# A Mamba block and a mixture of experts on one core: orders written out for head and tail, weights loaded at the start, and identity products on TensorE

## The reference

```python
xn = layernorm(x)
u, res = silu((xn @ W_in)[..., :256]), (xn @ W_in)[..., 256:]
delta = softplus(u @ W_delta + b_delta)
Bm, Cm = u @ W_B, u @ W_C                       # 16 states
h[t] = exp(delta[t] * A) * h[t-1] + delta[t] * Bm[t] * u[t]
y[t] = sum over the states of h[t] * Cm[t]
x = x + ((y + u * D) * silu(res)) @ W_out

xn = layernorm(x)
gate = xn @ Wg.T + bias; weights = softmax over the 4 largest of 8
out = swiglu(xn, Ws1, Ws2, Ws3) + sum over e of weights[e] * swiglu(xn, W1[e], W2[e], W3[e])
x = x + out                                     # hidden width 341 per expert
```

## Time and profile before

| what | us |
|---|---|
| median of three runs | 1600.95 (1597.64 to 1606.98) |
| profiled execution | 1600.77 |
| its span | 1598.9 |
| TensorE busy, whole span | 1466.7 (92%) |
| VectorE busy, whole span | 1443.5 (90%) |
| first scan of tile 0 starts | 47.77 |
| first `x1T` (tile 0's expert half begins) | 196.8 |

### The profile page before, as it was taken

How to read it: one execution, slowest core, us unless ns; L and a number is a source line. 1 busy time by engine, 2 the same in 40 slices (tenths; PEclk the granted TensorE clock), 3 DMA queues, 4 the chain that set the end, 5 groups by cost and what they waited for, 6 DMA issues and landing times.

```text
span 1598.9 us, 30425 instructions
## 1 busy us (share of the span) xinstructions
PE 1466.7 (92%) x9216; PEld 1210.6 (76%) x9216; DVE 1443.5 (90%) x2884; ACT 1210.7 (76%) x1789; POOL 848.4 (53%) x509
## 2 busy tenths in 40 slices
PE   3255699999999999999999999999999999999998
PEld 1133378878888887878888887878888798878887
DVE  0789899999999999999999999999999999998443
ACT  3464678888888888888888888978888888884332
POOL 1848474665546374665646385655737484661000
PEclk9567799999999999999999999999999999999999
DMA  4312121201212121201212121111212121100000
GB/s 149 112 41 79 41 80 41 74 14 47 81 41 87 41 87 41 71 16 40 86 41 86 40 83 38 55 38 40 86 41 86 41 79 36 64 23 10 6 7 7
DMA packets 50458, 86.97 MB, mean 54 GB/s; under 512 B 4647, under 2 KB 32804, under 8 KB 50340
## 3 DMA queue, kind: packets, MB, share of 16 engines
q1 hardware_dynamic: 50340, 85.66, 16.2%
HBM read 80.93 MB, written 4.72 MB: 54 GB/s over the span
## 4 chain that ended last, share of the span: by engine, by line
PE 57%; issue 14%; POOL 9%; DVE 8%; ACT 7%; DMA 2%; SPq 1%; DVEq 0%; POOLq 0%; ACTq 0%
PE eo_bank L889 18%; PE turn L836 8%; PE h L873 8%; PE h L875 7%; PE h L874 7%; POOL hb L452 5%; DVE hb L650 4%; PE side L800 3%; ACT L511 2%; PE side L813 2%; PE side L806 2%; DMA bbc<-b_rows 2%; DVE acc L662 2%; POOL soft L445 1%; POOL delta L440 1%
## 5 line engine op out<-in xcount | busy, mean ns | idle before, releaser
L452 POOL TENSOR_TENSOR hb<-soft,bbc 128x1024 f32<-128x1024 f32 x256 | 619.6, 2441 | 250.0 <-PE turn L836 207.5
L889 PEld LDWEIGHTS eo_bank<-w_sb,gated 128*128 128x128 f32 x3840 | 467.5, 192 | 34.8 <-issue 16.0
L889 PE MATMUL eo_bank<-w_sb,gated 128*128 128x128 f32 x3840 | 488.4, 276 | 5.0 <-DVE o L738 3.1
L662 DVE SCALAR_TENSOR_TENSOR acc<-turn,c_sb,acc 128x256 f32<-128x256 f32 x960 | 404.8, 471 | 10.2 <-PE turn L836 8.6
L511 ACT ACT_TABLE_LOAD x297 | 381.1, 1283 | 5.2
L836 PE MATMUL turn<-ident,hb 128*128 128x128 f32 x2048 | 313.6, 282 | 69.5 <-DVE acc L662 37.7
L836 PEld LDWEIGHTS turn<-ident,hb 128*128 128x128 f32 x2048 | 251.4, 145 | 130.8 <-issue 54.7
L594 ACT ACTIVATE s<-h 128x512 f32<-128x512 f32 x384 | 221.7, 596 | 150.9 <-PE h L875 144.0
L650 DVE TENSOR_TENSOR_SCAN hb<-decay,hb 128x512 f32<-128x512 f32 x256 | 330.2, 1317 | 5.0 <-issue 5.0
L650 DVE TENSOR_TENSOR_SCAN hb<-decay_bank,hb 128x512 f32<-128x512 f32 x256 | 310.0, 1211 | 20.5 <-POOL hb L452 13.5
L726 DVE TENSOR_TENSOR gated<-h,s 128x512 f32<-128x512 f32 x384 | 254.8, 676 | 47.3 <-PE h L875 35.1
(11 more groups left out here) (86 smaller groups left out, 1408.4 us busy)
## 6 DMA issues: line engine op xcount, KB each, us to landing
bbc<-b_rows SPq DMA_DIRECT2D x128, 512.0 KB, 5.7
x_in<-x_dram SPq DMA_DIRECT2D x16, 256.0 KB, 3.0
x_cur<-x_dram SPq DMA_DIRECT2D x16, 256.0 KB, 3.3
out_dram<-o SPq DMA_DIRECT2D x16, 256.0 KB, 2.4
gated<-w_all_dram SPq DMA_DIRECT2D x2, 1534.5 KB, 7.3
w_sb<-w_all_dram SPq DMA_DIRECT2D x5, 192.0 KB
b_rows<-cbT SPq DMA_DIRECT2D x16, 32.0 KB, 1.6
w_in_sb<-w_in_dram SPq DMA_DIRECT2D x1, 256.0 KB, 3.2
```

The costliest lines, as they stand in the source:

```text
L452: pool.tensor_tensor(hb[:, arg % HB_RING, :, :], du[:, h, :].unsqueeze(1).broadcast_to((P, GN, TOK)), bbc[:, r, :].rearrange("p (n t) -> p ...
L662: dve.scalar_tensor_tensor(acc[:, blk, :], turn_bank[pair][:, i * DI:(i + 1) * DI], c_sb[:, blk, n:n + 1], acc[:, blk, :], ALU.mult, ALU.add)\
L889: mm = pe.matmul(eo_bank[:, blk * P:(blk + 1) * P], gated[:, k % GATED_RING, blk * P:(blk + 1) * P], w3_sb[:, pair, :], start=(n == 0), st ...
```

## The change

There are five edits.

1. **Orders of their own.** The strings of the loop body stay as they are. Each engine gets two more strings, head and tail, with a tile number at each step, and `bodies` runs head, loop, tail. The loop now runs for j = 6 to 14, nine times in place of eight.
2. **One semaphore per kind of use of `side`,** in place of one for all.
3. **Early loads.** ScalarE issues W1 and W2 at its start, on its own DMA queue, W2 into a second staging buffer, `stage2`, which is the upper half of `hb`. `cut_hi` of W1 now follows `wi.1` of tile 0, `cut_hi` of W2 follows `soft`. VectorE makes both low parts one after the other after `c` of tile 0. GpSimd's `dbu` 4 to 7 of tile 0 wait until both are made. W3 is issued by SP after the last `bbc` of tile 0.
4. **Fewer waits at the start.** GpSimd waits no more for the small loads. VectorE negates A after `ln` of tile 0, not before, and only the first decays wait for it.
5. **Identity products.** TensorE multiplies the identity with itself (128 columns, fp32, into an expert bank that nobody reads yet): 16 times before it waits for the small loads, and then ahead of each step, until the first `h1`: 6 times ahead of `xT` and `dz`, 4 ahead of `bt`, 3 ahead of `wi` and `turn`, 2 ahead of the others.

```diff
+FILLERS = {"xT": 6, "dz": 6, "bt": 4, "wi": 3, "turn": 3}
+SP_HEAD = """
+0:load_x.0 0:b_out.0 0:bbc.0.1.2 0:load_cur.0 1:load_x.0 0:bbc.3 2:load_x.0 0:bbc.4.5.6.7 1:b_out.0
...
+PE_HEAD = """
+0:xT.0 0:wi.0.1 0:bt.0 0:dz.0.1 0:turn.0 0:ct.0 0:turn.1.2 0:wi_res.0.1 0:turn.3.4.5.6 1:xT.0 0:turn.7.8 1:wi.0
+0:turn.9.10.11.12.13 1:wi.1 0:turn.14.15 1:bt.0 0:turn.16 1:dz.0 0:turn.17 1:dz.1
+0:turn.18.19.20.21.22.23.24.25.26.27.28.29.30.31 1:turn.0 0:yT.0.1 1:turn.1 1:ct.0 1:turn.2 0:wo.0 1:turn.3
...
+2:bt.0 2:dz.0 1:turn.20 2:dz.1 1:turn.21.22.23.24 0:x1T.0 1:turn.25.26 0:h1.0.1 1:turn.27 0:h2.0 1:turn.28.29.30
...
+ACT_HEAD = """
+0:xn.0 0:xT.0 0:wi.0.1 0:bt.0 0:zb.0.1 0:soft.0 1:xn.0 0:decay1.0.1 0:ud.0 0:decay0.0 0:decay1.2.3.4
...
+DVE_HEAD = """
+0:ln.0 1:ln.0 0:scan0.0 0:scan1.0 2:ln.0 0:scan0.1 0:scan1.1 0:c.0 0:scan0.2 0:scan1.2 0:sum.2 0:scan0.3 0:sum.3
...
+POOL_HEAD = """
+0:rstd.0 1:rstd.0 0:delta.0 0:du.0 0:dbu.0.1.2.3.4.5.6.7.8.9.10.11.12.13.14.15 2:rstd.0 1:delta.0 1:du.0
...
+PE_TAIL = """
...
+13:h1.18 13:w3.20 13:h1.19 13:w3.21 15:turn.17 13:h2.19 13:w3.22.23 15:turn.18.19 13:h1.20.21 13:h2.20.21
...
+DVE_TAIL = """
...
+13:gated.22.23 14:xl.0 15:scan0.14 15:sum.24.25 15:scan0.15 15:scan1.14 14:gated.0 15:sum.26.27 15:scan1.15
...
+        stage2 = hb[:, HB_RING // 2:, :, :].rearrange("p r n t -> p (r n t)")[:, 0:HIDDEN]
...
+        def bodies(eng, engine, program):
+
+            head, body, tail = ORDER[engine]
+            program([((tile, 0), step, arg) for tile, step, arg in head], None)
             with eng.Fori(*LOOP) as j:
+                program([((j, SHIFT[part]), step, arg) for part, step, arg in body], body)
+            program([((tile, 0), step, arg) for tile, step, arg in tail], body)
...
-                        if isinstance(j, int) and j + SHIFT[part] == 0 and arg == 3:
-                            load_w2()
+                        if first(turn) and arg == NG - 1:
+                            load_w3()
...
+                        if first(turn) and HB_RING // 2 <= arg < HB_RING:
+                            pool.wait_ge(w_lo, 2)
...
-                    if isinstance(j, int) and j + SHIFT[part] == 0 and (step, arg) in (("zb", 1), ("decay1", 9)):
-                        cut_hi(step == "decay1")
+                    if first(turn) and (step, arg) in (("wi", 1), ("soft", 0)):
+                        cut_hi(step == "soft")
...
+            act.wait_ge(blank, 2)
+            for dst, src, landed in ((stage_in, w1_all, w1_in), (stage2_in, w2_all, w2_in)):
+                act.dma_start(dst, src.rearrange("p (g c) -> p g c", g=GROUPS)).then_inc(landed, 16)
             act.wait_ge(small_in, 16 * SMALL)
             act.activation(a_sb[:, :, :], a_sb[:, :, :], ACT.Exp).then_inc(a_exped, 1)
...
+                    if first(turn) and step == "c":
+                        cut_lo(False)
+                        cut_lo(True)
...
+            def stay_busy(times):
+
+                for _ in range(times):
+                    pe.matmul(h_bank[0][:, 0:P], ident[:, :], ident[:, :], start=True, stop=True)
...
+                    if step == "h1":
+                        idle_bank = False
+                    if idle_bank:
+                        stay_busy(FILLERS.get(step, 2))
...
             pe.wait_ge(consts, CONSTS)
+            stay_busy(16)
             pe.wait_ge(small_in, 16 * SMALL)
```

More of the change, by code:

```diff
@@ L124, in mamba_moe_kernel @@
     NT = x.shape[0] * x.shape[1] // TOK
-    steps = orders()
-    SIDE = ("xT", "wi", "wi_res", "dz", "bt", "ct", "yT", "wo", "x1T", "gate")
+    SIDE = {"xT": 1, "wi": NH, "wi_res": NH, "dz": NH, "bt": 1, "ct": 1, "yT": NH, "wo": 1, "x1T": 1, "gate": 1}
     SHIFT = {"f": 1, "m": 0, "e": -1, "d": -2, "c": -3, "b": -4, "a": -5}
[L131 to L153, removed]
+    LOOP = (1 - min(SHIFT[part] for engine in ORDER for part, _, _ in ORDER[engine][1]), NT - 1)
     ctx = ExitStack()
@@ L344, in load_small, with program @@
                     sp_eng.dma_start(w3_by_group[lo - k * P:hi - k * P, :, n, :], w3_of[lo:hi, :, :]).then_inc(w3_in, 16)
[L346 to L355, removed]
+            def program(entries, before):
+                for turn, step, arg in entries:
                     at = TT * turn[0] + TT * turn[1]
@@ L494, in normalize, with table_after, program @@
                                    scale=rstd[norm][:, i:i + 1]).then_inc(xn_ready[norm], 1)
[L496 to L508, removed]
+            def table_after(entries, table):
+                used = [TABLE_OF[step] for _, step, _ in entries if step in TABLE_OF]
+                return used[-1] if used else table
+            def program(entries, before):
+                table = table_after(before, None) if before else EXP_TABLE
+                head = before is None
+                for turn, step, arg in entries:
                     if TABLE_OF.get(step, table) != table:
@@ L535, in program @@
                         wait_before(act, zb_ready, turn, NH, 0)
[L536 removed]
+                        read_side(turn, step, arg, u[:, arg, :], side[:, :], ACT.Silu, wi_ready)
                     elif step == "ud":
@@ L628, in cut_lo, with program @@
                 hi, lo = (w2h, w2l) if second else (w1h, w1l)
[L629 to L634, removed]
-                    turn = turn_of(j, part)
+                dve.tensor_tensor(lo[:, :], stage2 if second else stage, hi[:, :].bitcast(F32), ALU.subtract).then_inc(w_lo, 1)
+            def program(entries, before):
+                for turn, step, arg in entries:
                     if step == "ln":
```

376 lines of the change are left out of this document (269 added, 107 removed).

## The result

Nine runs of the changed kernel gave a median of 1592.96 us (1591.1 to 1597.27), nine of the kernel before 1601.61 us: ratio 0.9948, interval 0.9932 to 0.9963. It is 8.6 us faster, where 18 us were forecast. The profiled execution took 1592.96 us, span 1591.2, against 1600.77 and 1598.9.

What follows compares the result with a forecast made beforehand. It took VectorE and TensorE, both near full, to bound the kernel, with gains at the start, head and tail: 14.0 us up to x1T plus 4.0 in the tail, 1600.8 - 18.0 = 1582.8 us, range 1572 to 1598.

Steps and rivals of the forecast that it cites:

- The start: Chain up to the first scan: scan at 42 us in place of 47.8, 5.8 us earlier, bounds 37 to 50.
- I put the small loads 1 us later: Start: W1 and W2 travelling at the same time delay the small loads by 1 us; xn starts at 9.9.
- x_in of tile 1: Start: this DMA, now later in SP's order, lands near 32 us and makes delta and the scan 4.5 us later.
- The clock at the start: Start: identity products bring the high clock, saving xT 0.45, wi 1.2 and 0.4, bt 1.8, dz.0 1.9 us.
- I put the gaps at 8 in place of 14.2: Head, first scan to x1T of tile 0: VectorE's waits shrink to 8 us from 14.2, bounds 3 and 18.
- 2 us per tile: Head: three products and a turn take 1.08 us against 0.94 for two sums, costing 2 us per tile.
- The forecast of 141 us: Head, first scan to x1T of tile 0: 132.8 us of work plus 8 of gaps, in place of 149.
- GpSimd's hold and the low parts: Head: holding GpSimd at dbu.4 costs nothing; W1's low part, no longer slowed by it, saves 2 us.
- The tail: Last Mamba tile: a tail order of its own takes back TensorE's gaps, 4.0 us, bounds -2 and 8.
- the head stays as slow as it was: Rival: small loads or x_in 4 us or more late, VectorE's waits stay at 14; 1596 us, chance 0.16.
- The third rival: Head: identity products run at the low clock, a turn with three takes 2.2 us; 1640 us, chance 0.06.
- The second: Rival, more is gained: x_in lands early, scan at 38, gaps 4, tail 7; 1574 us, chance 0.11.

Runs made afterwards that it cites:

- Experiment 1: The changed kernel with W1 and W2 issued by ScalarE only once the ten small loads are in: 1584.67 us, ratio 0.9894 to the kernel before.
- Experiment 2: The changed kernel with W1 and W2 after the small loads, and x_in of tile 1 issued before b_out and bbc of tile 0: 1580.34 us.
- experiment 11: The kernel before with identity products only at the beginning and ahead of xT, wi, bt and dz of tile 0: 1600.07 us, ratio 0.9990.
- experiment 7: The changed kernel with the head's bodies (j = -1 to 5) in the order of the loop: 1596.26 us, ratio 0.9974 to the kernel before.
- Experiments 3 to 5: The changed kernel with no identity products (1588.91 us), none ahead of turn (1587.84 us), or products only up to dz of tile 0 (1588.56 us).
- experiment 8: The changed kernel with weights after small loads, x_in of tile 1 earlier, and products only up to dz of tile 0: 1576.45 us, ratio 0.9836.

## Why the prediction was wrong, by its own steps

**The start: wrong, by one term.** The step "I put the small loads 1 us later" is the one that failed. They were 8.5 us later, near the bound of 9.4 that I had worked out and set aside, because "the ten small loads are issued from 1.2 us on". Being issued isn't being through: many of the ten have descriptors of 64 bytes and less. The DMA records in the trace show what happened. From 8 to 13 us there are 489 records on SP's queue, nearly all of 64 bytes, and 489 on ScalarE's, nearly all of 4092: one for one. In that time the small loads moved 0.04 MB and the weights 1.94. In the kernel before, from 4 to 6 us, SP's queue had 1311 records in 2 us. Even SP's issue of a 4 KB load took 3.08 us. Experiment 1 takes this delay away and gives 7.5 us in the trace and 8.3 in the time. The Trainium skill (DMA: Bandwidth & Descriptors, Queues, rings and completion order) has the engines take turns a packet at a time, and the trace agrees that they take turns. What was wrong is my working, which made of it a fair share by bytes. It gave 2.9 us, where 8.5 were measured for both weights and 4.5 for one. It also took 0.9 MB for the ten small loads, which by the sizes of their issues are 0.7 MB; that makes a share by bytes still smaller. From `xn` to the first scan the forecast had 32.1 us (9.9 to 42) and the trace has 32.2: the two misses of the next paragraphs, one each way, leave nothing of note there, which is luck.

**x_in of tile 1: right.** The mechanism was right, the size a little large: softplus ended at 38.7, `delta` started at 41.97, 3.2 us later, where the forecast had 4.5. Experiment 2 gave 2.8 us back in the scan.

**The clock at the start: mechanism right, size too large.** From `xn` to the scan the kernel before took 35.7 us, the changed one 32.2, and 34.6 without products: 2.4 us by the clock, where I had 5.75. Two reasons can be read. The late small loads left TensorE idle from 8 to 17 us, so `xT` ran at the low clock again (1.02 us against 0.66 in experiment 1). And where `bt` is slow, the cut of W1 hides most of it, and the wait for x_in of tile 1 hides what is left. In experiment 11, where the small loads are not late and no cut stands beside `bt`, it is 3.4 us; there `wi.0` still ran at the low clock, and x_in of tile 1 held `delta` back by 0.8 us.

**The head from the scan on: wrong.** "I put the gaps at 8 in place of 14.2"; they were 14.5 up to the same point. The price of a `turn` with three products was right (1.08 forecast, 1.11 measured; at the low clock 2.2 forecast, 2.16 measured). The decays' part shrank (6.9 down to 2.6), but not by the head's order alone: with the loop's order it is 2.9 (experiment 7). What failed is the count: I let the products slow only long runs of sums, "2 us per tile", and gave the high clock credit for shorter waits. Experiments 3 to 5 put the products at 5.4 to 7.4 us of this stretch, net of what the higher clock gives. No run has the clock of 0.90 without the products ahead of `turn`, so what it is worth by itself stays open; it did not pay for them.

The forecast of 141 us is what the kernel reaches without the products (141.0 and 141.2), but partly by luck. The waits are 9.5 us then, not 8. The work between the waits shrank by more than the 2 us forecast: counted to the low part of x1, from 139.4 to 133.2 us in the changed kernel, 1.6 us by the low part of W1 and 4.8 by the scans from the ring, which no term of the sum had.

**GpSimd's hold and the low parts: right.** W1's low part took 3.73 us in place of 5.32, and nobody waited for GpSimd after its release.

**The tail: right.** 4 us forecast, 4.5 measured. The loop didn't move. From `x1T` to the end the trace shows 6.8 us less, not 4.5; 2.6 of it come from the mark, which now stands closer to the use of its result. Counted from the low part of x1 it is 4.2 us.

**The rivals.** What happened is the first one, "the head stays as slow as it was", by both of its conditions, small loads over 4 us late and waits still at 14. It was given 1596 us and 0.16; the time came out 3 us lower, since the tail gave 4.2 us and not 2, and the scans 4.8. The third rival's mechanism occurred in short stretches, as for the `turn` near 131 us. The second had 1574 us, and 1575 was reached once the two faults were removed, but by other terms: the scan at 37, as it said, while the waits of the head were 12.0 us in experiment 8, where it had 4, and the tail gave 4, where it had 7.

**What stays open.** Experiment 11 is 3.4 us shorter up to `x1T` in its trace, and its median is not lower by as much; the interval of its ratio reaches down to 0.9976, 3.8 us, so the times don't rule it out. Why the waits for the decays fell with the loop's order too. And what edits 2 and 4 give by themselves: neither was run alone.

## What to carry to other kernels

A large load started early on a second queue isn't free for the small loads that everything waits for: start it right behind them. Work put in to keep TensorE's clock up has to end before the step is due: in a chain that another engine paces, ahead of every step it costs its full length each time steps follow closely, and here the higher clock did not pay for it. When a start moves, look at each DMA whose place in the queue moved with it, and at whoever waits for it in the order of an engine.

## What the hardware did that was not expected

3.14 MB of 4092-byte descriptors on ScalarE's queue delayed 0.7 MB of shorter ones on SP's queue by 8.5 us, the two queues advancing one record for one, and SP's issue of one 4 KB load took 3.08 us in place of 0.47. A scan of VectorE whose decays lie in the ring took 1.20 us alone and up to 3.3 us beside a GpSimd operation of 128 x 1024 elements; one whose decays lie in a PSUM bank took 1.21 us either way.
